# Writing out the first and last four turns of a software-pipelined kernel as one interleaved list per engine

## The chip, the cores and the metric

One core of one Trainium2 chip. The metric is device time in microseconds (us), from launch to the end of the program; the median over runs is what is compared.

## The reference

The input x is 32 sequences of 256 rows of 128 numbers, float32. Four layers follow each other, each as x = layer_norm(x + layer(x)):

```python
x = _layernorm(x + attn0(x))   # A: linear attention, 8 heads, RoPE, 5-tap conv of v, gate
x = _layernorm(x + ffn0(x))    # B: base matmul + the top-1 of four low-rank adapters
x = _layernorm(x + attn1(x))   # C: causal softmax attention, one head
x = _layernorm(x + ffn1(x))    # R, D: top-4 of 16 experts (grouped) + a shared expert, SwiGLU
```

## The kernel before, in words

The rows are cut into 16 blocks of 512 (two sequences, four tiles of 128 rows). Each block passes through the stages A, B, C and D; `r_` pieces (the router) belong to stage D's expert choice, and `e_norm` is the last layer norm with the store behind it. Each stage is split into small pieces, one function for each piece and engine: `a_xT_` to `a_out` are PE's pieces of stage A, `a_rope`, `conv_tap`, `a_mix`, `a_res` DVE's, and so on. A piece waits on semaphores for its inputs and for the buffers that it overwrites, then issues one to twelve instructions. The same name on two engines is one step seen from both.

The loop is software-pipelined over 20 turns. Turn i holds stage A of block i, B of i - 1 (with the projections of C), C and the router of i - 2, D of i - 3 and the last norm's input of i - 4. `turn(i)` exists once for each engine and lists the pieces in a fixed, hand-written order; `live(n)` leaves out pieces of blocks that don't exist. So turn 0 has A(0) alone, turn 1 A(1) and B(0), turn 2 A(2), B(1), C(0), turn 3 A(3), B(2), C(1), D(0); turns 4 to 15 are complete; turns 16 to 19 run empty again, down to the last norm of block 15. Everything is unrolled: there is no loop on the chip, and each engine works its list strictly in order.

Most buffers exist once. Stage A uses the PSUM banks A0 and A1, stages B, C and the router B0 and B1, stage D the banks GB (gate), UB (up), CB (routing weights) and YB (sum). So the next block's `a_xT_` waits for this block's `a_mix` (A0), its `a_vT_` for this block's `a_res` (A1). D's inner chain is, for chunk c of nine: `d_hidden` (six matmuls into GB and UB), `d_silu` on ACT, `d_gu` and `d_hid` on DVE, `d_down` on PE; a `d_hidden` waits for the `d_silu` and the `d_gu` of the chunk before.

POOL has the `ln_of(k, n)` pieces: eleven tiny instructions that make mean and rstd of layer norm k from DVE's statistics. `split_late` (ACT, then DVE) splits the expert weights into a high and a low part; it runs once, and D(0) needs it.

In the order before, POOL's `turn` puts `x0_lo(i)`, on which `a_vT_(i)` waits, ahead of `a_rope(i)`, but behind `ln_of(0, i - 1)` of the turn before; PE's puts `a_out(i)` behind `c_xT(i - 1)`, and `a_num_`, `a_aT`, `a_out` between the chunks of D:

```python
                if d: d_hidden(i - 3, 1 - odd, 8)
                if b: c_xT(i - 1)
                if a: a_out(i)
                if d: d_down(i - 3, 7)
                if b: c_project(i - 1)
```

Of the kernel before, what the change touches and what calls it, by code (L numbers as in the profile page):

```python
# [111 lines left out]
def build(nc, x_dram, weight_dram, whole_dram, out_dram):  # L112
    blocks = x_dram.shape[0] // BLOCK
    turns = blocks + 4
    assert blocks % 2 == 0
# [1162 lines left out]
```

## Time and profile before

| | us |
|---|---|
| median of 3 runs (lowest, highest) | 721.76 (721.19, 721.92) |
| profiled execution, its own time | 720.15 |
| span of the profile | 718.4 |
| busy: PE, DVE, ACT, POOL | 657.7, 586.9, 485.1, 308.9 |

The profiled execution lies 1.61 below the median, and 1.75 of its time lie outside the span (launch and end). The page cuts the span into 40 slices of 18 us; PE's row shows 3, 4, 6, 6, 6 and 7 tenths in the first six slices, 9 (90% or more) from there on, and 4 in the last. Turn boundaries can be read off PE's timeline: `c_value` is PE's last piece of a turn. Turn 3 ends at 142.1 and turn 15 at 619.6. The span therefore splits into a first part of 142.1 (turns 0 to 3), twelve steady turns of 477.5 together (39.79 each), and a last part of 98.8 (turns 16 to 19).

### The profile page before, as it was taken

The page shows a single profiled execution, that of the slowest core. Times are in us where ns is not written, and L with a number is a line of the kernel's source. Part 1 is how long each engine was busy: PE and PEld are TensorE (multiplying, and loading weights), DVE is VectorE, ACT ScalarE, POOL GpSimd, SP SyncE. Part 2 cuts the span into 40 slices and gives each one's busy share as a digit, 9 for nine tenths or more (in the row PEclk, how much of TensorE's full clock was granted, in tenths as well). Part 3 has the DMA queues.
Part 4 walks back from the last instruction along what each step waited for, and adds up shares of the span by engine and source line. Part 5 has one row for each costly group of instructions (what it writes and reads, how often), then busy time and mean ns, then how long its engine had stood idle before and what let it go on. Part 6 is the DMA issues. An engine that isn't in the chain of part 4 may idle for free.

```text
span 718.4 us, 11716 instructions
## 1 busy us (share of the span) xinstructions
PE 657.7 (92%) x3654; PEld 508.2 (71%) x3654; DVE 586.9 (82%) x1873; ACT 485.1 (68%) x978; POOL 308.9 (43%) x793
## 2 busy tenths in 40 slices
PE   3466679999999999999999999999999999999994
PEld 2354558787878777787878787787868787766652
DVE  1566778989898888989899888989898998877672
ACT  2233558587787878687787877786877868676623
POOL 1234443445453544536454535446454535250311
PEclk9787989999999999999999999999999999999997
DMA  6000000000000010101000000101000000000000
GB/s 227 15 1 16 1 16 0 16 1 16 16 16 16 1 31 1 31 1 30 1 17 16 10 21 2 30 1 31 2 28 3 16 1 1 15 1 16 16 1 29
DMA packets 18686, 12.69 MB, mean 18 GB/s; under 512 B 704, under 2 KB 18240, under 8 KB 18368
## 3 DMA queue, kind: packets, MB, share of 16 engines
q1 hardware_dynamic: 18624, 11.95, 5.4%
q8 instruction: 29, 0.48, 0.3%
q14 instruction: 33, 0.27, 0.1%
HBM read 7.75 MB, written 4.19 MB: 17 GB/s over the span
## 4 chain that ended last, share of the span: by engine, by line
PE 87%; DVE 5%; POOL 3%; ACT 3%; issue 1%; DMA 1%; SPq 0%; ACTq 0%; DVEq 0%; POOLq 0%
PE bank L551 17%; PE bank L346 11%; PE bank L348 10%; PE bank L347 10%; PE bank L355 10%; PE bank L461 2%; PE bank L434 2%; PE bank L472 2%; PE bank L478 2%; PE bank L473 2%; PE bank L406 2%; PE bank L518 2%; PE bank L449 2%; PE bank L424 2%; PE bank L505 1%; PE bank L499 1%
## 5 line engine op out<-in xcount | busy, mean ns | idle before, releaser
L551 PE MATMUL bank<-hid,whole 128*128 128x512 f32 x288 | 147.2, 593 | 0.8 <-DVE hid L1055 0.8
L346 PE MATMUL bank<-x3T_hi,w_hi 128*128 128x512 f32 x288 | 138.0, 479 | 1.8 <-DVE gu L1052 1.4
L728 ACT ACTIVATE silu<-bank 128x512 f32<-128x512 f32 x144 | 86.3, 600 | 66.1 <-PE bank L348 62.9
L1052 DVE TENSOR_TENSOR gu<-silu,bank 128x512 f32<-128x512 f32 x128 | 86.7, 677 | 35.3 <-ACT silu L728 18.8
L348 PE MATMUL bank<-x3T_hi,w_lo 128*128 128x512 f32 x288 | 113.5, 394 | 0.0
L347 PE MATMUL bank<-x3T_lo,w_hi 128*128 128x512 f32 x288 | 112.7, 391 | 0.0
L1151 POOL TENSOR_TENSOR moment<-stats 128x4 f32<-128x4 f32 x192 | 44.7, 265 | 149.3 <-DVE stats L866 133.8
L1062 DVE TENSOR_TENSOR hid<-gu,bank 128x512 f32<-128x512 f32 x128 | 87.2, 681 | 1.8 <-PE bank L551 0.8
L346 PEld LDWEIGHTS bank<-x3T_hi,w_hi 128*128 128x128 f32 x288 | 54.2, 188 | 30.8 <-ACT silu L728 9.8
L1137 POOL TENSOR_TENSOR qk<-rope_c,rope_s 128x512 f32<-128x512 f32 x32 | 40.6, 1279 | 80.8 <-DVE rope_s L828 80.8
L1151 POOL TENSOR_TENSOR rstd<-moment,whole 128x4 f32<-128x4 f32 x64 | 64.6, 1009 | 5.0
L347 PEld LDWEIGHTS bank<-x3T_lo,w_hi 128*128 128x128 f32 x288 | 54.5, 189 | 16.3 <-issue 10.0
L348 PEld LDWEIGHTS bank<-x3T_hi,w_lo 128*128 128x128 f32 x288 | 54.0, 188 | 12.2
L551 PEld LDWEIGHTS bank<-hid,whole 128*128 128x128 f32 x288 | 49.7, 189 | 15.3 <-issue 7.2
L1181 POOL TENSOR_TENSOR x3T_lo<-x3T,x3T_hi 128x512 fp32r<-128x512 f32 x16 | 22.0, 1372 | 87.9 <-ACT x3T_hi L718 87.9
L728 ACT ACT_TABLE_LOAD x45 | 57.7, 1283 | 0.8
L939 DVE SCALAR_TENSOR_TENSOR conv<-vT,whole,conv 128x512 f32<-128x512 f32 x64 | 54.3, 849 | 0.8
L866 DVE BATCH_NORM_STATS2 stats<-res 128x6 f32<-128x128 f32 x192 | 41.9, 281 | 1.7
L1151 POOL TENSOR_TENSOR moment<-moment,whole 128x4 f32<-128x4 f32 x192 | 35.2, 199 | 5.0
L355 PE MATMUL bank<-whole,x 128*128 128x128 f32 x192 | 30.0, 280 | 7.6 <-ACT x L634 7.2
L355 PEld LDWEIGHTS bank<-whole,x 128*128 128x128 f32 x192 | 23.7, 144 | 18.6 <-ACT x L634 8.1
L634 ACT ACTIVATE x<-bank,shift,rstd 128x128 f32<-128x128 f32 x64 | 24.1, 456 | 18.7 <-POOL shift L1151 18.7
(196 smaller groups left out, 1634.4 us busy)
## 6 DMA issues: line engine op xcount, KB each, us to landing
x_in<-x SPq DMA_DIRECT2D x16, 256.0 KB, 2.7
out<-x SPq DMA_DIRECT2D x16, 256.0 KB, 2.3
whole<-w_whole SPq DMA_DIRECT2D x1, 1198.5 KB, 5.4
w_raw<-w SPq DMA_DIRECT2D x1, 1152.0 KB
w_raw<-w SPq DMA_DIRECT2D x1, 546.0 KB, 6.7
whole<-w_whole SPq DMA_DIRECT2D x16, 32.0 KB
whole<-w_whole SPq DMA_DIRECT2D x1, 64.0 KB
```

The lines of the kernel that those rows point to most:

```text
L346: mm(out, wh, mh, start=True, stop=False)
L347: mm(out, wh, ml, start=False, stop=False)
L348: return mm(out, wl, mh, start=False, stop=True)
L355: last = nc.tensor.transpose(out[0:parts, t * P:(t + 1) * P], src(t), eye)
L551: mm(YB[:], whole[:, a:a + P], hid[:, c % 2], start=c == 0, stop=c == CHUNKS).then_inc(p_w2.sem, 1)
L728: fn(silu[:, c % 2], GB[:], ACT.Silu).then_inc(a_silu.sem, 1)
L866: nc.vector.bn_stats(stats[k][:, t, :], res[k][:, t, :]).then_inc(v_st[k].sem, 1)
L939: stt(conv[:], vT[:, :, j:j + SEQ], taps[:, j:j + 1], conv[:], ALU.mult, ALU.add).then_inc(v_conv.sem, 1)
L1052: tt(gu[:, c % 2], silu[:, c % 2], UB[:], ALU.mult).then_inc(v_gu.sem, 1)
L1062: tt(hid[:, c % 2], gu[:, c % 2], CB[:], ALU.mult).then_inc(v_hid.sem, 1)
L1137: tt(qk[:, 2 * h:2 * h + 2, :].rearrange("p t d -> p (t d)"), rope_c[:, h], rope_s[:, h], ALU.add).then_inc(g_qk.sem, 1)
L1151: tt(out, in0, in1, op).then_inc(g_ln[k].sem, 1)
```

## The change

The function `turn` stays as it is, but is called for turns 4 to 15 alone. Turns 0 to 3 are replaced on each engine by `first_turns()`, turns 16 to 19 by `last_turns()`: straight lists of the same pieces, each exactly once, in an order in which pieces of several blocks are mixed. No piece crosses from one of the three parts into another. PE's `a_qT_`, which reads what POOL's `a_rope` writes, gets a wait of its own, because in the new first list `a_qT_(2)` and `a_qT_(3)` stand ahead of `a_kv`, which had the wait before.

```diff
             def a_qT_(n):
                 pe.wait_ge(a_g.sem, a_g.at(n))
+                pe.wait_ge(g_qk.sem, g_qk.at(n))
                 transpose_tiles(A0, lambda t: qk[:, t, 0:P], ident).then_inc(p_qT.sem, 1)
...
-            for i in range(turns):
+            def first_turns():
+                a_xT_(0, 0, 0)
+                a_vT_(0)
+                a_qk(0)
...
+            def last_turns():
+                d_hidden(13, 1, 0)
+                c_scores(14)
...
+            first_turns()
+            for i in range(4, 16):
                 turn(i, i % 2, i // 2)
+            last_turns()
```

The lists themselves, in order, written without brackets: `d_hidden 0,2` is chunk 2 of block 0, `ln_of 2,0` the layer norm 2 of block 0; a name with several arguments is that piece called several times; the arguments that choose one of two buffers are left out.

```
PE first_turns (90 calls)
a_xT 0; a_vT 0; a_qk 0; a_g 0; a_v 0; a_kv 0; a_qT 0; a_num 0; a_aT 0; a_xT 1; a_out 0; a_vT 1; a_qk 1; b_xT 0;
b_small 0; a_v 1; a_g 1; a_kv 1; a_qT 1; a_num 1; b_dnT 0; b_up 0; a_aT 1; a_xT 2; a_out 1; c_xT 0; a_vT 2; c_project
0; c_value 0; c_scores 0; a_qk 2; c_pT 0; b_xT 1; c_av 0; a_g 2; a_qT 2; a_v 2; b_small 1; r_xT 0; a_kv 2; r_gate 0;
b_dnT 1; b_up 1; a_num 2; d_hidden 0,0; a_aT 2; d_hidden 0,1; a_xT 3; a_out 2; c_xT 1; c_project 1; c_value 1; a_vT 3;
a_qk 3; c_scores 1; d_cT 0; a_g 3; a_v 3; c_pT 1; d_down 0,0; c_av 1; a_qT 3; d_hidden 0,2; d_down 0,1; b_xT 2;
d_hidden 0,3; b_small 2; a_kv 3; d_down 0,2; r_xT 1; d_hidden 0,4; r_gate 1; d_down 0,3; d_hidden 0,5; a_num 3; b_dnT
2; d_hidden 0,6; b_up 2; d_down 0,4; d_hidden 0,7; a_aT 3; d_hidden 0,8; d_down 0,5 0,6; a_out 3; c_xT 2; d_down 0,7;
c_project 2; d_down 0,8; c_value 2
PE last_turns (78 calls)
d_hidden 13,0; c_scores 14; d_yT 12; d_cT 13; c_pT 14; d_hidden 13,1; c_av 14; b_xT 15; d_down 13,0; b_small 15;
d_hidden 13,2 13,3; d_down 13,1; d_hidden 13,4; r_xT 14; d_down 13,2; r_gate 14; d_down 13,3; d_hidden 13,5; b_dnT 15;
d_down 13,4; b_up 15; d_hidden 13,6; d_down 13,5; d_hidden 13,7; d_down 13,6; d_hidden 13,8; c_xT 15; d_down 13,7
13,8; d_hidden 14,0; c_project 15; c_value 15; d_hidden 14,1; c_scores 15; d_cT 14; d_yT 13; c_pT 15; d_down 14,0;
c_av 15; d_hidden 14,2; d_down 14,1; d_hidden 14,3; d_down 14,2; d_hidden 14,4; d_down 14,3; d_hidden 14,5; r_xT 15;
d_hidden 14,6; r_gate 15; d_down 14,4; d_hidden 14,7; d_down 14,5; d_hidden 14,8; d_down 14,6 14,7 14,8; d_hidden
15,0; d_yT 14; d_cT 15; d_hidden 15,1 15,2 15,3; d_down 15,0 15,1; d_hidden 15,4; d_down 15,2 15,3; d_hidden 15,5;
d_down 15,4; d_hidden 15,6; d_down 15,5; d_hidden 15,7; d_down 15,6; d_hidden 15,8; d_down 15,7 15,8; d_yT 15
ACT first_turns (66 calls)
x0_hi 0; a_vT 0; a_g 0; a_v 0; a_tap0 0; a_qT 0; x0_hi 1; a_vT 1; split_late; a_tap0 1; copy_xT 0,1; b_small 0; a_v 1;
a_g 1; b_exp 0; a_qT 1; b_dnT 0; b_layer_norm 0; x0_hi 2; copy_xT 0,2; c_qkv 0; a_vT 2; c_exp 0; c_pT 0; a_g 2; a_tap0
2; copy_xT 1,1; b_small 1; a_qT 2; a_v 2; c_norm 0; b_exp 1; r_hi 0; r_exp 0; b_dnT 1; d_silu 0,0; b_layer_norm 1;
x0_hi 3; copy_xT 1,2; d_silu 0,1; c_qkv 1; a_vT 3; a_tap0 3; c_exp 1; c_pT 1; a_g 3; d_silu 0,2; copy_xT 2,1; a_v 3;
d_silu 0,3; b_small 2; c_norm 1; a_qT 3; r_hi 1; d_silu 0,4; b_exp 2; r_exp 1; d_silu 0,5; b_dnT 2; d_silu 0,6 0,7;
b_layer_norm 2; copy_xT 2,2; d_silu 0,8; c_qkv 2; d_y 0
ACT last_turns (51 calls)
d_silu 13,0; c_exp 14; c_pT 14; d_silu 13,1; copy_xT 15,1; d_silu 13,2; b_small 15; e_norm 12; d_silu 13,3; c_norm 14;
d_silu 13,4; r_hi 14; r_exp 14; b_exp 15; d_silu 13,5; b_dnT 15; d_silu 13,6 13,7; b_layer_norm 15; d_silu 13,8;
copy_xT 15,2; d_silu 14,0; c_qkv 15; d_y 13; d_silu 14,1; c_exp 15; c_pT 15; d_silu 14,2 14,3 14,4; c_norm 15; d_silu
14,5; r_hi 15; d_silu 14,6; r_exp 15; d_silu 14,7 14,8 15,0; d_y 14; e_norm 13; d_silu 15,1 15,2 15,3 15,4 15,5;
e_norm 14; d_silu 15,6 15,7 15,8; d_y 15; e_norm 15
DVE first_turns (98 calls)
a_rope 0; conv_tap 0,1; a_kv 0; conv_tap 0,2 0,3; a_den 0; a_att 0; conv_tap 0,4; a_mix 0; a_res 0; a_layer_norm 0;
a_rope 1; b_norm 0,0 0,1; b_logits 0; b_first 0; a_kv 1; b_weigh 0; conv_tap 1,1 1,2 1,3 1,4; b_res 0; a_den 1; a_att
1; a_mix 1; a_res 1; split_late; c_value 0; c_max 0; a_layer_norm 1; a_rope 2; c_res 0; b_norm 1,0 1,1; b_logits 1;
conv_tap 2,1; b_first 1; b_weigh 1; conv_tap 2,2; r_groups 0,0; a_kv 2; r_groups 0,1; conv_tap 2,3; r_groups 0,2;
conv_tap 2,4; r_groups 0,3; b_res 1; a_den 2; a_att 2; d_gu 0,0; a_mix 2; r_groups 0,4; a_res 2; r_combine 0; c_value
1; a_rope 3; c_max 1; d_hid 0,0; d_gu 0,1; conv_tap 3,1 3,2; d_hid 0,1; a_layer_norm 2; c_res 1; d_gu 0,2; d_hid 0,2;
d_gu 0,3; d_hid 0,3; b_norm 2,0 2,1; conv_tap 3,3 3,4; a_kv 3; d_gu 0,4; b_logits 2; b_first 2; b_weigh 2; d_hid 0,4;
r_groups 1,0; d_gu 0,5; a_den 3; r_groups 1,1 1,2; d_hid 0,5; d_gu 0,6; b_res 2; a_att 3; d_hid 0,6; d_gu 0,7;
r_groups 1,3; a_mix 3; d_hid 0,7; r_groups 1,4; a_res 3; d_gu 0,8; r_combine 1; c_value 2
DVE last_turns (79 calls)
c_max 14; d_gu 13,0; d_res 12; d_hid 13,0; a_layer_norm 15; c_res 14; d_gu 13,1; d_hid 13,1; d_gu 13,2; d_hid 13,2;
b_norm 15,0; d_gu 13,3; b_norm 15,1; d_hid 13,3; b_logits 15; d_gu 13,4; d_hid 13,4; b_first 15; b_weigh 15; r_groups
14,0 14,1; d_gu 13,5; d_hid 13,5; b_res 15; d_gu 13,6; d_hid 13,6; d_gu 13,7; d_hid 13,7; r_groups 14,2 14,3; d_gu
13,8; r_groups 14,4; r_combine 14; d_gu 14,0; c_value 15; c_max 15; d_hid 14,0; d_res 13; d_gu 14,1; d_hid 14,1; c_res
15; d_gu 14,2; d_hid 14,2; d_gu 14,3; d_hid 14,3; d_gu 14,4; d_hid 14,4; d_gu 14,5; d_hid 14,5; d_gu 14,6; r_groups
15,0; d_hid 14,6; r_groups 15,1 15,2 15,3; d_gu 14,7; r_groups 15,4; d_hid 14,7; d_gu 14,8; r_combine 15; d_gu 15,0;
d_hid 15,0; d_gu 15,1; d_hid 15,1; d_gu 15,2; d_res 14; d_hid 15,2; d_gu 15,3; d_hid 15,3; d_gu 15,4; d_hid 15,4; d_gu
15,5; d_hid 15,5; d_gu 15,6; d_hid 15,6; d_gu 15,7; d_hid 15,7; d_gu 15,8; d_res 15
POOL first_turns (26 calls)
x0_lo 0; a_rope 0; a_gate 0; x0_lo 1; ln_of 0,0; a_rope 1; b_norm 0; ln_of 1,0; a_gate 1; x0_lo 2; ln_of 0,1; a_rope
2; ln_of 2,0; b_norm 1; x3_lo 0; ln_of 1,1; a_gate 2; x0_lo 3; ln_of 0,2; a_rope 3; ln_of 2,1; b_norm 2; x3_lo 1;
ln_of 1,2; a_gate 3; ln_of 0,3
POOL last_turns (10 calls)
ln_of 3,12 2,14; b_norm 15; ln_of 1,15; x3_lo 14; ln_of 2,15 3,13; x3_lo 15; ln_of 3,14 3,15
```

## Rows read from the trace of the kernel before

**Rows 1.** Busy time of each engine by stretch; x counts instructions, PEclk is the granted clock

```profile
0.00:32.70 32.70, 13.31 (x65) 10.94 (x66) 10.84 (x31) 7.93 (x18) 6.93 (x13) 0.93 0.37 125
32.70:67.30 34.60, 20.35 (x105) 15.99 (x104) 21.07 (x59) 12.70 (x28) 13.97 (x36) 0.72 0.06 16
67.30:102.10 34.80, 22.80 (x149) 18.59 (x147) 24.34 (x88) 16.06 (x42) 14.99 (x37) 0.90 0.03 8
102.10:142.10 40.00, 39.96 (x228) 31.00 (x228) 35.09 (x115) 30.03 (x58) 16.50 (x41) 1.00 0.03 8
...
142.10:619.60 477.50, 477.50 (x2737) 374.83 (x2736) 430.96 (x1393) 365.37 (x732) 233.09 (x589) 1.00 0.05 13
619.60:718.40 98.80, 83.77 (x380) 56.87 (x379) 64.55 (x189) 53.06 (x101) 23.40 (x81) 0.96 0.04 11
...
706.00:718.40 12.40, 2.36 (x8) 0.71 (x6) 2.08 (x6) 2.24 (x5) 2.76 (x11) 0.70 0.07 21
```

**Rows 2.** Who waited for whom, 0 to 142 us: total, times, longest

```profile
ACT x L634 <- POOL shift L1151: 13.2, 3, 6.9
```

**Rows 3.** POOL's timeline in turn 1

```profile
36.45 1.03 POOL L1151 TENSOR_TENSOR rstd<-moment,whole 128x4 f32<-128x4 f32 x1
37.45 1.26 POOL L1176 TENSOR_TENSOR x0T_lo<-x0T,x0T_hi 128x512 fp32r<-128x512 f32 x1
```

**Rows 4.** DVE's timeline in the first part: start, length, what

```profile
37.51 2.05 DVE L871 TENSOR_SCALAR x<-res,mean,rstd 128x128 f32<-128x128 f32 x4 [3.02 <-POOL rstd L1151]
41.73 0.69 DVE L826 TENSOR_TENSOR rope_c<-bank,whole 128x512 f32<-128x512 f32 x1 [2.16 <-PE bank L394]
...
56.93 0.88 DVE L859 SCALAR_TENSOR_TENSOR mixT<-bank,neg_mean,conv 128x256 f32<-128x256 f32 x2 [1.21 <-PE bank L355]
...
63.44 0.69 DVE L876 TENSOR_TENSOR res<-x_in,bank 128x512 f32<-128x512 f32 x1 [1.90 <-PE bank L434]
...
72.72 0.69 DVE L826 TENSOR_TENSOR rope_c<-bank,whole 128x512 f32<-128x512 f32 x1 [1.51 <-PE bank L394]
...
92.56 0.88 DVE L859 SCALAR_TENSOR_TENSOR mixT<-bank,neg_mean,conv 128x256 f32<-128x256 f32 x2
...
98.90 0.69 DVE L876 TENSOR_TENSOR res<-x_in,bank 128x512 f32<-128x512 f32 x1 [2.90 <-PE bank L434]
...
110.26 0.69 DVE L826 TENSOR_TENSOR rope_c<-bank,whole 128x512 f32<-128x512 f32 x1 [1.50 <-PE bank L394]
...
143.06 0.68 DVE L999 TENSOR_TENSOR cv<-bank,whole 128x512 f32<-128x512 f32 x1
```

**Rows 5.** PE's timeline in turns 1 and 3

```profile
38.76 0.79 PE L346 MATMUL bank<-x0T_hi,w_hi 128*128 128x512 f32 x1 [5.05 <-POOL x0T_lo L1176]
...
60.58 1.11 PE L355 MATMUL bank<-whole,x 128*128 128x128 f32 x4 [3.69 <-ACT x L634]
...
109.27 0.36 PE L392 MATMUL bank<-w_hi,x0T_hi 128*128 128x256 f32 x1
```

**Rows 6.** DVE's timeline, two operations that appear short and long

```profile
57.72 1.22 DVE L806 TENSOR_TENSOR w_lo<-w_raw,w_hi 128x1024 fp32r<-128x1024 f32 x1
...
59.05 2.29 DVE L806 TENSOR_TENSOR w_lo<-w_raw,w_hi 128x1024 fp32r<-128x1024 f32 x1
...
107.65 1.11 DVE L871 TENSOR_SCALAR x<-res,mean,rstd 128x128 f32<-128x128 f32 x4
```

**Rows 7.** PE's timeline in the last part

```profile
665.85 0.50 PE L346 MATMUL bank<-x3T_hi,w_hi 128*128 128x512 f32 x1 [1.23 <-DVE gu L1052]
...
687.15 0.66 PE L355 MATMUL bank<-whole,comb 128*128 128x128 f32 x4 [0.96 <-DVE comb L1045]
```

**Rows 8.** Groups of instructions: busy, mean ns, idle before and its releaser

```profile
L728 ACT ACT_TABLE_LOAD x45 | 57.7, 1283 | 0.8
...
L355 PE MATMUL bank<-whole,v_cent 128*128 128x128 f32 x64 | 9.9, 277 | 0.4 <-DVE rope_s L828 0.4
...
L355 PE MATMUL bank<-whole,qk 128*128 128x128 f32 x64 | 9.6, 273 | 0.0
```

More of the change, by code:

```diff
@@ L765, in turn, with first_turns @@
                 if d: d_y(i - 3)
-            for i in range(turns):
+            def first_turns():
+                x0_hi(0)
+                a_vT_(0)
+                a_g_(0)
+                a_v_(0)
+                a_tap0(0)
+                a_qT_(0)
+                x0_hi(1)
+                a_vT_(1)
+                split_late()
+                a_tap0(1)
+                copy_xT(0, 1, B0)
+                b_small(0)
+                a_v_(1)
+                a_g_(1)
+                b_exp(0)
+                a_qT_(1)
+                b_dnT(0)
+                b_layer_norm(0)
+                x0_hi(2)
+                copy_xT(0, 2, B0)
+                c_qkv(0)
+                a_vT_(2)
+                c_exp(0)
+                c_pT(0)
+                a_g_(2)
+                a_tap0(2)
+                copy_xT(1, 1, B0)
+                b_small(1)
+                a_qT_(2)
+                a_v_(2)
+                c_norm(0, 0)
+                b_exp(1)
+                r_hi(0, 0)
+                r_exp(0)
+                b_dnT(1)
+                d_silu(0, 0)
+                b_layer_norm(1)
+                x0_hi(3)
+                copy_xT(1, 2, B0)
+                d_silu(0, 1)
+                c_qkv(1)
+                a_vT_(3)
+                a_tap0(3)
+                c_exp(1)
+                c_pT(1)
+                a_g_(3)
+                d_silu(0, 2)
+                copy_xT(2, 1, B0)
+                a_v_(3)
+                d_silu(0, 3)
+                b_small(2)
+                c_norm(1, 1)
+                a_qT_(3)
+                r_hi(1, 1)
+                d_silu(0, 4)
+                b_exp(2)
+                r_exp(1)
+                d_silu(0, 5)
+                b_dnT(2)
+                d_silu(0, 6)
+                d_silu(0, 7)
+                b_layer_norm(2)
+                copy_xT(2, 2, B0)
+                d_silu(0, 8)
+                c_qkv(2)
+                d_y(0)
@@ L768, in _ @@
+            first_turns()
+            for i in range(4, 16):
                 turn(i, i % 2)
+            last_turns()
         @block.vector
@@ L1120, in _ @@
+            first_turns()
+            for i in range(4, 16):
                 turn(i, i % 2)
+            last_turns()
         @block.gpsimd
@@ L1193, in turn, with first_turns, last_turns @@
                 if a: ln_of(0, i)
-            for i in range(turns):
+            def first_turns():
+                x0_lo(0)
+                a_rope(0)
+                a_gate(0)
+                x0_lo(1)
+                ln_of(0, 0)
+                a_rope(1)
+                b_norm(0)
+                ln_of(1, 0)
+                a_gate(1)
+                x0_lo(2)
+                ln_of(0, 1)
+                a_rope(2)
+                ln_of(2, 0)
+                b_norm(1)
+                x3_lo(0, 0)
+                ln_of(1, 1)
+                a_gate(2)
+                x0_lo(3)
+                ln_of(0, 2)
+                a_rope(3)
+                ln_of(2, 1)
+                b_norm(2)
+                x3_lo(1, 1)
+                ln_of(1, 2)
+                a_gate(3)
+                ln_of(0, 3)
+            def last_turns():
+                ln_of(3, 12)
+                ln_of(2, 14)
+                b_norm(15)
+                ln_of(1, 15)
+                x3_lo(14, 0)
+                ln_of(2, 15)
+                ln_of(3, 13)
+                x3_lo(15, 1)
+                ln_of(3, 14)
+                ln_of(3, 15)
+            first_turns()
+            for i in range(4, 16):
                 turn(i, i % 2)
+            last_turns()
 def _constants():
```

395 lines of the change are left out of this document (394 added, 1 removed).

## The prediction

> **What bounds the kernel now.** Read the table by stretches first [rows 1]. In the twelve steady turns PE is busy for all of 477.5 us, at full clock. They keep their order, so nothing can be won there; the change must be judged in the two stretches around them. In the last 98.8 us PE is busy for 83.77, so it idles for 15.0. Of these 10.0 (12.40 less 2.36) lie in the very end, where block 15's sum goes through the last transposition, the layer norm and the store; no order shortens that. So the last part has little to give. The first 142.1 us are different: turns 0, 1 and 2 are 32.7, 34.6 and 34.8 us long, with PE busy for 13.31, 20.35 and 22.80, and DVE for 10.84, 21.07 and 24.34. No engine is the bound there. They are long because each engine walks its list in order and waits. Turn 3 (40.0 us) is full already: PE 39.96, DVE 35.09.
>
> The waits say for what [rows 2, 5]: in the first part ACT waits 13.2 us in three `b_layer_norm` for POOL's shift, and PE's matmuls of `a_vT_(1)` wait 5.05 for POOL's x0T_lo. Both are chains through POOL's small layer-norm instructions. What counts is whether such a chain holds up work that doesn't need it, by standing ahead of it in a list. I therefore walked through the new lists by hand, piece by piece on the four engines, with the durations of the trace, and compare six marks on DVE with before; DVE sees every step of stage A.
>
> **Turn 1.** Before, POOL does x0T_lo of block 1 right behind rstd of block 0, at 37.45 [rows 3], so `a_vT_(1)` starts at 38.76 [rows 5] and `a_rope(1)` at 41.73 [rows 4]. The new list of POOL has `x0_lo(1)` ahead of `ln_of(0, 0)`, and PE has `a_xT_(1)` ahead of `a_out(0)`; `a_vT_(1)` can go once block 0's `a_res` has freed A1, at about 32.8. But DVE keeps `a_layer_norm(0)` ahead of `a_rope(1)`, and that needs rstd. So the rope comes from this chain: rstd ends at 36.45 + 1.03 = 37.5, about 0.9 earlier since one conv tap has moved behind `a_att(0)`; then the norm, 1.11 where POOL is idle [rows 6]: 37.7, which is 4.0 earlier. From there to `a_mix(1)` took 15.2 (41.73 to 56.93) [rows 4]; I take 16.2, because ACT's `split_late` now stands ahead of `a_tap0(1)` and x1T's copy. Mix at 53.9, 3.0 earlier. Then the clear gain: PE had `a_out(1)` behind `c_xT(0)`, which waited 3.69 for the norm on ACT [rows 5], and `a_res(1)` came 6.5 after the mix [rows 4]. Now `a_out(1)` stands ahead and only POOL's norm and gate lie between: 4.0. `a_res(1)` at 57.9, 5.5 earlier.
>
> **Turn 2.** From `a_res(1)` to `a_rope(2)` took 9.3 (63.44 to 72.72) [rows 4]; now 10.3, because DVE's `split_late` and C(0)'s `c_value` and `c_max` stand between. Rope at 68.2, 4.5 earlier. From there to `a_mix(2)` took 19.8 and does again: B(1), the first router pieces and the conv taps are reordered, and `d_gu(0, 0)` is fitted in. Mix at 88.0, 4.6 earlier. `a_out(2)` is pulled ahead of `c_xT(1)` as in turn 1: `a_res` follows the mix after 3.85 instead of 6.34, at 91.85, 7.0 earlier.
>
> **Turn 3.** `a_rope(3)` came 11.36 after `a_res(2)` (98.90 to 110.26) [rows 4]; between stood the router's `r_combine(0)`, `c_value`, `d_gu`, `c_max`, `d_hid` and a layer norm. Now only the statistics (0.8), `r_combine(0)` (3.6) and `c_value(1)` (0.6) do: 5.8 with the start-ups. `a_vT_(3)` and `a_qk(3)` are done on PE by 98.2, so the rope goes at 97.65 on its first half, 12.6 earlier. From here both engines are nearly full. DVE: before, 33.5 from this rope to the end of `c_value(2)` (110.26 to 143.74) [rows 4]; to this come `c_max(1)`, `d_hid(0, 0)` and the norm of block 2, which were done before and now follow, 2.9 together; and I find 2.1 of waits more than before, at `d_gu(0, 3)`, `d_gu(0, 4)` (ACT's Silu behind `c_norm(1)`) and `d_hid(0, 7)`. 97.65 + 33.5 + 2.9 + 2.1 = 136.2 against 143.74: **7.5 earlier**. PE: 40.0 of turn 3, less what it has done by the end of `a_qk(3)`. Before, `a_qk(3)` starts 7.2 into the turn [rows 1, 5]; of that, 3.0 (`c_scores`, `d_cT`, `c_pT`) still lie ahead, and `a_qk` itself takes 1.5: 40.0 - 4.2 - 1.5 = 34.3, so PE can't end before 98.2 + 34.3 = 132.5, 9.6 earlier than 142.1. My walk puts its end at 134.0, 8.1 earlier. I take the later engine, 7.5. The steady turns then start 7.5 earlier and are what they were.
>
> **The last part.** Here PE has two waits of size, 1.23 for `d_gu` and 0.96 for `comb` of block 15 [rows 7]; by the walk the first goes, as `d_hidden(14, 0)` and `(14, 1)` now stand around C(15), and the second stays at about 0.5. Against it, `b_exp(15)` now stands behind `r_exp(14)`, which costs 0.4, and the router of block 15 comes one chunk later. Net 1.1 earlier; bounds 0 and 5.0 (15.0 less 10.0 that PE idles at the end).
>
> **Edits at nothing.** The added wait: in the steady turns `a_kv` stands ahead of `a_qT_` with the same count, so it is met when PE arrives; behind it stand the four transpositions and `d_hidden` 2 or 3. For its own price, the four transpositions of v_cent behind two waits take 277 ns each, those of qk behind one 273 [rows 8]: 12 turns x 4 x 0.004 = 0.2 us at most, and 0 is nearer, since a piece with a met wait shows no gap. If the cover were gone, the wait would be for POOL's two additions; in `first_turns` it is really waited for, and the walk has it. Exp and Silu now change places less often: I count 7 table loads in turn 3 and 10 in the last part before, 5 and 8 after. Four loads of 1283 ns [rows 8] are 5.1 us of ACT, hidden as ACT is busy 30.03 of 40.0 in turn 3 [rows 1]; at most the 1.0 of the wait at `d_gu(0, 4)` would come back without them.
>
> **The sum.** 7.5 + 1.1 = 8.6. Against the profiled execution: 720.15 - 8.6 = 711.6. That execution lay 1.61 below the median, so the median comes to 721.76 - 8.6 = **713.2**.
>
> **Rivals.**
> - *DVE gets slower where it is packed* (0.20). Some DVE operations appear short and long: the layer norm's four 1.11 and, beside x0T_lo on POOL, 2.05; the split 1.22 and, beside POOL's product oT, 2.29 [rows 3, 4, 6]. I took the short ones. If the two norms that were short and the first half of the split meet POOL's large additions, that is 2 x 0.94 + 1.07 = 3.0 on DVE's path: gain 5.6, time 716.2. For it: POOL has more to do in the same time. Against: behind `ln_of` in POOL's list mostly a wait follows. The Trainium skill (GPSIMD Engine Reference, section Specifications) says that GpSimd shares SBUF interfaces with VectorE, with contention for VectorE instructions with two SBUF inputs or in a 2-port mode. The trace agrees for these two operations, with 2.05 against 1.11 and 2.29 against 1.22.
> - *The last part fills up too* (0.08): 7.5 + 5.0 = 12.5, time 709.3. Against it: D's chunks hang on each other there and nothing else is left to put between.
> - *Given back in turn 3* (0.06). The lead of 12.6 at `a_rope(3)` is worth only what PE and DVE can take up; if DVE waits for 9 us there instead of 2.1, say because each Silu of D(0) sits on ACT behind a norm or an Exp that is late, the first part wins 0.6: about 720.5 to 722, no change.
> - *Slower: the clock* (0.04). Turns 1 and 2 ran at a granted clock of 0.72 and 0.90, with PE busy for 59 and 66% [rows 1]. If D(0), taken apart among waits, ran at 0.72, PE's 34.3 would take 47.6 and end at 145.8: 3.7 later, less 1.1, time 724.4. It decides from a clock below 0.76 in this stretch. Against: turn 3 ran at 1.00, and by the walk PE is busy for 34.3 of 35.8 us.
>
> **How the numbers follow.** The forecast, a gain of 6.5 to 11, has 0.62, and its own range is 710.8 to 715.3. A measurement of this kernel can tell 0.2%, 1.4 us. Faster by more: 0.62 + 0.20 + 0.08 = 0.90; within: 0.06; slower: 0.04. For 8 in 10 the range goes up past the first rival, to 718.5, and down nearly to the second, to 709.0; the rest lies outside.
>
> **What will show it.** On DVE `a_res(1)` near 58, `a_res(2)` near 92, `a_rope(3)` near 98, `c_value(2)` ending near 136; PE's `c_value(2)` ending near 134, the twelve steady turns at 477.5, and 97.7 behind them. 86 table loads in place of 90. The prediction is wrong if `a_rope(2)` isn't earlier than 71 (the pieces put ahead of it cost more than the waits that they fill), if DVE waits more than 5 us between `a_rope(3)` and `c_value(2)`, or if the steady turns lengthen.

## The result, and the profile after

The changed kernel takes 709.65 us (median of 4 runs, 707.79 to 711.87) beside 721.48 for the kernel before (720.89 to 721.92): a ratio of 0.9838, 95% interval 0.9805 to 0.9871. The profiled execution took 708.59 us, with a span of 706.8.

Marked by the end of PE's `c_value`, which closes a turn, the two spans compare like this:

| stretch | before | after | gain | predicted |
|---|---|---|---|---|
| start to the end of `c_value(2)` | 142.09 | 133.09 | 9.00 | 7.5 |
| to the end of `c_value(14)` (twelve steady turns) | 477.50 | 477.63 | -0.13 | 0 |
| to the end of the last `d_down` | 88.11 | 85.43 | 2.68 | 1.1 |
| the very end | 10.66 | 10.65 | 0.01 | 0 |
| span | 718.4 | 706.8 | 11.6 | 8.6 |

The first row rests on PE's `c_value(2)`, before and after; a matmul group's start plus its length is its end:

```profile
141.04 1.05 PE L478 MATMUL bank<-w_raw,x2T 128*128 128x128 f32 x8
```

```profile
132.04 1.05 PE L479 MATMUL bank<-w_raw,x2T 128*128 128x128 f32 x8
```

The windows of the changed kernel answer to [rows 1]; columns as there.

```profile
28.00:55.20 27.20, 18.90 (x86) 16.03 (x86) 15.02 (x51) 9.45 (x21) 10.80 (x25) 0.69 0.04 11
55.20:91.40 36.20, 29.04 (x174) 24.19 (x175) 26.87 (x84) 20.16 (x49) 19.37 (x41) 0.83 0.03 8
91.40:132.93 41.53, 40.25 (x225) 29.76 (x223) 37.03 (x128) 26.79 (x56) 18.04 (x48) 1.00 0.05 14
132.93:610.49 477.56, 477.56 (x2739) 374.76 (x2737) 431.35 (x1394) 365.32 (x732) 232.81 (x589) 1.00 0.05 13
```

From 91 us on PE is nearly full, earlier than before. Ahead of it, in 63.4 us, it is busy for 47.94 and at a granted clock of 0.69 and 0.83, lower than turns 1 and 2 had before (0.72 and 0.90). The busy time there is partly slow time. Over the whole first part the two profiles are alike in this: the mean granted clock is 0.89 in 142.09 us before and 0.88 in 133.09 us after, so about 31 us at half clock (0.50, the lower of the two levels in the records; the other is 1.00) in either. Less time at half clock is not where the gain comes from; where that time falls is taken up below.

DVE's timeline of the changed kernel, the marks of [rows 4]:

```profile
37.04 1.12 DVE L1169 TENSOR_SCALAR x<-res,mean,rstd 128x128 f32<-128x128 f32 x4 [3.02 <-POOL rstd L1632]
38.07 0.68 DVE L1124 TENSOR_TENSOR rope_c<-bank,whole 128x512 f32<-128x512 f32 x1
...
55.16 0.88 DVE L1157 SCALAR_TENSOR_TENSOR mixT<-bank,neg_mean,conv 128x256 f32<-128x256 f32 x2 [1.15 <-PE bank L355]
59.56 0.69 DVE L1174 TENSOR_TENSOR res<-x_in,bank 128x512 f32<-128x512 f32 x1 [3.52 <-PE bank L435]
...
67.85 0.68 DVE L1124 TENSOR_TENSOR rope_c<-bank,whole 128x512 f32<-128x512 f32 x1
...
87.84 0.88 DVE L1157 SCALAR_TENSOR_TENSOR mixT<-bank,neg_mean,conv 128x256 f32<-128x256 f32 x2
...
91.43 0.69 DVE L1174 TENSOR_TENSOR res<-x_in,bank 128x512 f32<-128x512 f32 x1 [0.18 <-PE bank L435]
...
97.05 0.68 DVE L1124 TENSOR_TENSOR rope_c<-bank,whole 128x512 f32<-128x512 f32 x1
...
134.41 0.68 DVE L1297 TENSOR_TENSOR cv<-bank,whole 128x512 f32<-128x512 f32 x1
```

| mark | before | predicted | after |
|---|---|---|---|
| `a_rope(1)` | 41.73 | 37.7 | 38.07 |
| `a_mix(1)` | 56.93 | 53.9 | 55.16 |
| `a_res(1)` | 63.44 | 57.9 | 59.56 |
| `a_rope(2)` | 72.72 | 68.2 | 67.85 |
| `a_mix(2)` | 92.56 | 88.0 | 87.84 |
| `a_res(2)` | 98.90 | 91.85 | 91.43 |
| `a_rope(3)` | 110.26 | 97.65 | 97.05 |
| `c_value(2)` on DVE ends | 143.74 | 136.2 | 135.09 |
| `c_value(2)` on PE ends | 142.09 | 134.0 | 133.09 |

In the last part the 1.23 at `d_gu` and the 0.96 at `comb` of [rows 7] are gone. Five waits of PE are left ahead of the very end, the largest 0.48, the others 0.31 to 0.34; two of them:

```profile
671.08 1.98 PE L552 MATMUL bank<-hid,whole 128*128 128x512 f32 x4 [0.34 <-DVE hid L1360]
...
674.92 0.66 PE L355 MATMUL bank<-whole,yT 128*128 128x128 f32 x4 [0.48 <-ACT yT L907]
```

The runs of the changed kernel lie 4 us apart, those of the kernel before that were timed with it 1 us; over all sets below the latter go from 720.9 to 723.4. The runs go with their mean granted clock, which the experiments take up.

### The profile page after: what moved, and what is told of

It is laid out like the page before. It is cut to its first block, busy times and chain, and to the rows that moved or that the text cites. A ratio compares the mean times of both kernels' runs of the same rounds, so it can differ in the third digit from the quotient of the medians.

```text
span 706.8 us, 11728 instructions
## 1 busy us (share of the span) xinstructions
PE 662.7 (94%) x3654; PEld 510.9 (72%) x3654; DVE 585.6 (83%) x1873; ACT 479.4 (68%) x974; POOL 310.7 (44%) x793
## 4 chain that ended last, share of the span: by engine, by line
PE 88%; ACT 4%; DVE 3%; POOL 2%; issue 1%; DMA 1%; SPq 0%; ACTq 0%; DVEq 0%; POOLq 0%
PE bank L552 17%; PE bank L346 11%; PE bank L348 10%; PE bank L347 10%; PE bank L355 10%; PE bank L462 2%; PE bank L435 2%; PE bank L406 2%; PE bank L479 2%; PE bank L425 2%; PE bank L473 2%; PE bank L474 2%; PE bank L450 2%; PE bank L519 2%; PE bank L500 1%; PE bank L506 1%
## 5 line engine op out<-in xcount | busy, mean ns | idle before, releaser
L1632 POOL TENSOR_TENSOR moment<-stats 128x4 f32<-128x4 f32 x192 | 46.5, 274 | 151.9 <-DVE stats L1164 124.6
L552 PEld LDWEIGHTS bank<-hid,whole 128*128 128x128 f32 x288 | 49.5, 189 | 16.2 <-issue 7.4
L1657 POOL TENSOR_TENSOR x0T_lo<-x0T,x0T_hi 128x512 fp32r<-128x512 f32 x16 | 20.3, 1270 | 36.6 <-ACT x0T L815 36.6
```

Of the source, the lines that this page charges most:

```text
L552: mm(YB[:], whole[:, a:a + P], hid[:, c % 2], start=c == 0, stop=c == CHUNKS).then_inc(p_w2.sem, 1)
L1632: tt(out, in0, in1, op).then_inc(g_ln[k].sem, 1)
```

## The experiments

Each experiment was timed against the kernel before on the same chip, in five sets. The medians of the kernel before in these sets lie between 721.5 and 722.3, so a comparison with the 709.65 of the changed kernel, which belongs to another set, is uncertain by some 0.8 us beside the spread of the runs.

**The two halves by themselves.** `first_only`:

```diff
-            for i in range(4, 16):
+            for i in range(4, turns):
...
-            last_turns()
```

> The new lists for turns 0 to 3, the old order in the last four turns. By the two profiles PE's c_value(2) ends 9.1 us earlier in the first part, the steady turns are 0.3 longer, and the last part gives 2.7: this kernel then is 9.1 - 0.3 = 8.9 us faster than the kernel before (712.6 beside 721.5), with the last part at 99.1 us again. The rival is the prediction's own sum, 7.5 for the first part; what is above it in the profile would belong to a good moment of the granted clock, and this kernel would come out at 714.0.

Measured: 710.27 us (710.20 to 711.21) beside 721.62, ratio 0.9841 (0.9828 to 0.9855). Its profiled execution took 711.21 us, 8.9 less than that of the kernel before (720.15), as expected: `c_value(2)` ends at 133.01, the last part takes 88.14. But the kernel's other runs lie 0.9 us below its profiled one, and those of the kernel before 1.0 to 3.0 above its own, so the medians differ by 11.4. The median itself, 710.27, is 2.3 below the expected 712.6. The first part is worth 8.9 in one pair of profiles and 11.4 in the medians; the rival's 7.5 is below both.

`last_only`:

```diff
-            first_turns()
-            for i in range(4, 16):
+            for i in range(16):
```

> The old order in turns 0 to 15 (with the added wait in each a_qT_), the new list for the last four turns. By the two profiles the last part goes from 99.05 to 96.3 us, since PE's waits there for block 14's and 15's pieces go from 5.0 to 1.8: 2.7 us faster than before, 718.8. The rival is the prediction's 1.1, 720.4; then the rest of the 2.7 would come from how the lists of the first part meet those of the last, or from the clock.

Measured: 718.61 us (718.45 to 720.34) beside 721.62, ratio 0.9959 (0.9946 to 0.9973), 3.0 us faster; the last part takes 85.35 in its profile. The 2.7 belong to the new list of the last four turns, whatever stands ahead of it. In the eleven profiles with that list unchanged the part takes 85.32 to 85.43. This profile shows one thing more: its turns 0 to 3 are in the old order, as in the kernel before, and yet its `c_value(2)` ends at 143.11, 1.0 later. The mean clock of that stretch is 0.87, beside 0.89:

```profile
0.00:143.11 143.11, 98.37 (x540) 78.65 (x541) 91.45 (x293) 66.72 (x145) 51.88 (x125) 0.87 0.12 37
```

So the profile of the kernel before, with its 142.09, was one of its quicker executions.

**The added wait.** `wait_four`:

```diff
-                pe.wait_ge(g_qk.sem, g_qk.at(n))
+                if n < 4: pe.wait_ge(g_qk.sem, g_qk.at(n))
```

> The whole change, but with the added wait in a_qT_ for blocks 0 to 3 alone, so that the twelve steady turns are as they were. By the prediction the added wait costs nothing there: the time is that of the changed kernel, 709.7, within 0.2, apart from the spread of the runs. The rival takes the 0.26 us by which the steady turns of the changed kernel were longer as the price of twelve waits: 0.3 less. It is also a second sample of the changed kernel: if its runs spread over 4 us too and lie higher where the mean granted clock is lower, the spread belongs to the new lists and not to one bad run.

Measured: 708.44 us (706.09 to 711.59), ratio 0.9812 (0.9789 to 0.9836). From the end of `c_value(2)` to that of `c_value(14)` it takes 477.58, with the twelve waits 477.63. A price of 0.05 can't be told from none: the other profiles with the twelve waits take 477.50 to 477.70, the kernel before without them 477.50. Its five runs, with the four of the changed kernel, form one series of mean granted clock and time: 0.983: 706.09; 0.978: 707.36, 707.79; 0.975: 708.44; 0.973: 708.48, 708.59; 0.971: 710.71; 0.969: 711.59, 711.87. So the 4 us of the changed kernel were not one bad run, and they go with the clock. That is a correlation; what the clock costs is tried below, by holding it. Nor is all of the spread new: the kernel before has 2.1 us in this set (721.10 to 723.17).

**Is it the chain, or the pieces of turn 3 put into turn 2?** `turn3_old` takes out of the four lists what belongs to turn 3 and runs that turn by the old loop:

```diff
-                d_hidden(0, 0, 0)
                 a_aT(2)
-                d_hidden(0, 0, 1)
-                a_xT_(3, 1, 1)
                 a_out(2)
                 c_xT(1)
...
-            for i in range(4, 16):
+            for i in range(3, 16):
```

> The new lists for turns 0 to 2 without any piece of turn 3, then turn 3 in the old order, and the new last four turns. By the prediction's steps block 2's a_res is still about 7 us earlier than before (near 91.5), and PE then has the 40.0 us of turn 3 whole, from about 95.5: c_value(2) ends near 135.6 in place of 132.9, so 2.7 later than the changed kernel, near 712.3. The rival: the early gaps were worth little by themselves, and the gain of the first part is that D(0) and A(3) are mixed into turn 2; then half or more of it is lost, 4.5 us or more, 714 and up.

Measured: 713.65 us (712.56 to 713.85) beside 721.62. `a_res(2)` is at 91.85, where it should be, but PE's `c_value(2)` ends at 138.32, 5.2 later than in the changed kernel, where the prediction's steps give 2.7: by the profiles it is the rival's number. The medians lie 4.0 apart, between the two. PE's timeline of this kernel shows why:

```profile
86.65 0.65 PE L355 MATMUL bank<-whole,att 128*128 128x128 f32 x4 [1.44 <-DVE att L1080]
89.74 2.08 PE L435 MATMUL bank<-whole,oT 128*128 128x128 f32 x8 [2.43 <-POOL oT L1512]
...
93.35 2.07 PE L473 MATMUL bank<-x2T,w_raw 128*128 128x512 f32 x2 [0.69 <-ACT x2T L762]
95.22 1.91 PE L474 MATMUL bank<-x2T,w_raw 128*128 128x512 f32 x2
96.92 1.61 PE L479 MATMUL bank<-w_raw,x2T 128*128 128x128 f32 x8
```

Its window from 91.4 to 98.5 has a granted clock of 0.53:

```profile
91.40:98.50 7.10, 6.41 (x20) 3.90 (x20) 4.74 (x22) 2.60 (x4) 2.62 (x10) 0.53 0.14 38
```

Where D(0)'s matmuls stood, PE now waits for 1.44 and 2.43, and then `a_out(2)` to `c_value(1)` run at half clock, 89.74 to 98.53, 8.8 us; in the changed kernel 90.24 to 95.58, 5.3:

```profile
90.24 1.16 PE L435 MATMUL bank<-whole,oT 128*128 128x128 f32 x8 [0.62 <-POOL oT L1624]
...
94.42 1.16 PE L479 MATMUL bank<-w_raw,x2T 128*128 128x128 f32 x8
```

Whether the clock or the missing work costs the 5.2 was tried next: `turn3_warm` puts work into those waits that serves nothing, here against `turn3_old`.

```diff
+            def warm(k):
+                for _ in range(k):
+                    nc.tensor.transpose(GB[:, 0:P], ident, ident)
...
+                warm(5)
                 a_aT(2)
+                warm(9)
                 a_out(2)
                 c_xT(1)
+                warm(2)
                 c_project(1)
```

> The kernel with turn 3 in the old order (713.65 us), and 16 extra transpositions of the identity into an unused bank, put into PE's list ahead of block 2's a_aT (5), a_out (9) and C(1)'s c_project (2), where PE waited 1.44, 2.43 and 0.69 us. They do no work of the kernel. If the 3.4 us by which a_out(2) to c_value(1) took longer there (8.8 against 5.3 in the changed kernel) came from the granted clock (0.53 in that stretch), which fell because PE had nothing to do in those waits, then those pieces now run at full clock, c_value(1) ends near 95 in place of 98.5, and the time is about 710.2. The rival: what was lost was D(0)'s and A(3)'s work itself, filling the waits; then idle transpositions bring nothing and the time is 713.6 or more.

Measured: 711.05 us (710.67 to 713.43), 2.6 below `turn3_old` and nearer to the expected 710.2 than to the rival's 713.6. The same pieces on PE:

```profile
90.64 1.16 PE L439 MATMUL bank<-whole,oT 128*128 128x128 f32 x8 [1.32 <-POOL oT L1519]
...
92.92 1.12 PE L477 MATMUL bank<-x2T,w_raw 128*128 128x512 f32 x2 [0.47 <-ACT x2T L769]
93.89 1.02 PE L478 MATMUL bank<-x2T,w_raw 128*128 128x512 f32 x2
94.83 1.16 PE L483 MATMUL bank<-w_raw,x2T 128*128 128x128 f32 x8
```

They take 5.35 us, the expected 3.4 less; 1.0 is given back because `a_mix(2)` came 1.0 later in this run (88.37 against 87.34). `c_value(2)` ends at 135.80, 2.5 earlier than in `turn3_old`. So of the 5.2, 2.5 came back with the clock in these profiles, and 3.4 would have without that delay: half to two thirds is the clock that D(0)'s early matmuls held up. That the rest is the work itself is what remains by subtraction; no run shows it.

**Single moves undone.** `out_behind`:

```diff
-                a_out(1)
                 c_xT(0)
+                a_out(1)
...
-                a_out(2)
                 c_xT(1)
+                a_out(2)
```

> The whole change, but with a_out(1) back behind c_xT(0) and a_out(2) back behind c_xT(1) on PE. By the prediction each of these moves brought about 2.5 us at the next a_res, so both a_res are late, block 1's by 2.5 (62.1) and block 2's by 5 (96.4), and the time is some 4 us longer, 713.6. The rival, from the profile of the changed kernel: ACT's norm for c_xT(0) ends at 57.45 there and POOL's product for a_out(1) at 57.39, and likewise at 90.5 and 90.2 in turn 2, so that the swap costs only the four transpositions, about 1.0 and 0.7: a_res at 60.6 and 93.1, the time 1 to 1.7 longer.

Measured: 712.61 us (709.04 to 714.75); runs so far apart can't decide between 713.6 and the rival's 710.7 to 711.4, the marks can. From `a_mix` to `a_res` it takes 4.87 and 4.39, in the changed kernel 4.40 and 3.59: the moves are worth 0.5 and 0.8, not 2.5 each. The profile is nevertheless 4.5 later at `c_value(2)`, since `a_mix(2)`, ahead of the second swap, comes at 91.55 instead of 87.84. Both kernels wait 3.6 us at `r_xT(0)`, to 78.0 and 77.9, and in both the clock falls. The window of `out_behind` in which it is low:

```profile
76.50:90.10 13.60, 11.42 (x48) 10.68 (x49) 9.51 (x35) 4.79 (x11) 3.91 (x12) 0.50 0.00 0
```

and that of the changed kernel:

```profile
74.70:81.50 6.80, 3.56 (x17) 3.56 (x17) 5.05 (x21) 3.86 (x9) 3.52 (x4) 0.50 0.00 0
```

The clock is at half for 13.6 us in one execution and for 6.8 in the other, where half of it falls into the wait. The same pieces behind the same wait therefore run at half clock for 12.1 us in one and 3.6 in the other. The 3.7 by which `a_mix(2)` is later are about what the runs of the changed kernel lie apart (4.1).

`lo_behind`, on POOL:

```diff
-                x0_lo(1)
                 ln_of(0, 0)
+                x0_lo(1)
...
```

and likewise `x0_lo(2)`, `x0_lo(3)` behind `ln_of(0, 1)`, `ln_of(0, 2)`.

> The whole change, but on POOL x0T_lo of blocks 1, 2 and 3 back behind the layer norm of the block before. By the prediction's first step POOL's order sets a_rope(1): x0T_lo then runs at 37.0 instead of 31.4, a_vT(1) starts 5 us later, at 38.3, a_rope(1) 3 us later, near 41, and in turn 2 a_vT(2) goes from 60.4 to about 66 with the pieces of C(0) queued behind it, a_rope(2) near 76, and the time 7 to 8.5 us longer, about 717.5: most of the gain is gone. The rival: the rope waits for POOL's rstd in any case and the rest is taken up by slack, so that only the 3 us of turn 1 are lost, 712.7.

Measured: 726.85 us (724.26 to 728.76), ratio 1.0069 (1.0045 to 1.0094): slower than the kernel before, and 9 us beyond the expected 717.5: neither number was near. `a_rope(1)` comes at 42.59, 4.5 later than in the changed kernel, `a_rope(2)` at 82.23, 14.4 later. Its POOL, PE and DVE timelines, one fence each:

```profile
71.20 1.01 POOL L1632 TENSOR_TENSOR rstd<-moment,whole 128x4 f32<-128x4 f32 x1
72.18 1.26 POOL L1657 TENSOR_TENSOR x0T_lo<-x0T,x0T_hi 128x512 fp32r<-128x512 f32 x1
```

```profile
73.50 0.79 PE L346 MATMUL bank<-x0T_hi,w_hi 128*128 128x512 f32 x1 [6.96 <-POOL x0T_lo L1657]
```

```profile
78.82 0.69 DVE L1297 TENSOR_TENSOR cv<-bank,whole 128x512 f32<-128x512 f32 x1 [8.85 <-PE bank L479]
```

Read from the top: POOL finishes the norm of block 1 before it makes x0T_lo of block 2; PE has `a_vT(2)` ahead of C(0) and waits 6.96; DVE has C(0)'s `c_value` ahead of the norm that block 1 needs and waits 8.85. In this kernel the new orders of PE and DVE only pay with POOL's. The clock has a part in it (0.961 to 0.966 in these runs, 0.969 to 0.978 in those of the changed kernel); how large, no run shows.

**The last part.** `last_av`:

```diff
                 c_pT(14)
+                c_av(14)
                 d_hidden(13, 1, 1)
-                c_av(14)
...
                 c_pT(15)
+                c_av(15)
                 d_down(14, 0)
-                c_av(15)
```

> The whole change, but in the last four turns c_av(14) and c_av(15) back directly behind c_pT(14) and c_pT(15) on PE, without d_hidden(13, 1) and d_down(14, 0) between them. Before, PE waited 0.63 us at each of the two; the prediction had only counted the waits of 1.23 and 0.96. If the 2.7 us of the last part are the sum of such small waits that got filled, these two come back: the last part (end of c_value(14) to the end of the last d_down, 85.3 to 85.4 us in the four profiles of the new list, 88.1 in two of the old one) becomes about 86.6, 1.2 longer. The rival: a wait that is opened here is made up at the next piece that waits for another engine, and the part stays within 0.3 of 85.4; then the 2.7 come from C(15) standing earlier as a whole.

Measured: 709.17 us (708.79 to 713.17); the times can't tell 1 us here, the profile can. The last part takes 86.80, 1.4 longer, and two waits stand in PE's timeline that the changed kernel doesn't have:

```profile
616.11 0.49 PE L506 MATMUL bank<-cv,probT 128*128 128x128 f32 x2 [0.58 <-ACT probT L874]
...
652.87 0.49 PE L506 MATMUL bank<-cv,probT 128*128 128x128 f32 x2 [0.58 <-ACT probT L874]
```

What is opened there is not made up later, and the rival's 0.3 is out.

**Further by order.** `tight` puts the nineteen pieces around turn 2 into another order on PE, and their partners elsewhere. The core on PE, without the lines that go further down in exchange:

```diff
                 a_v_(2)
+                a_qT_(2)
+                a_kv(2)
+                a_num_(2)
                 r_xT(0, 0)
+                a_aT(2)
...
                 b_up(1)
+                a_out(2)
                 d_hidden(0, 0, 1)
+                a_vT_(3)
+                a_qk(3)
                 c_xT(1)
```

> The whole change, and in turn 2 the pieces are moved further: on PE a_kv(2) and a_num(2) ahead of r_xT(0), into the wait of 3.62 us there, a_out(2), a_vT(3) and a_qk(3) ahead of c_xT(1); on ACT x1T's copy ahead of a_g(2) and x0T_hi(3) ahead of the Silus; on DVE block 2's kv_m, den and att ahead of b_logits(1) with the conv taps in its waits, and a_rope(3) ahead of c_value(1); on POOL a_gate(2) and x0T_lo(3) ahead of the norm of x1(1). If the chain of stage A through turn 2 is what holds the first part, a_mix(2) goes from 87.8 to about 81 and a_rope(3) from 97 to about 91; from there PE is the bound, which idled some 7 us between 55 and 91 and ran at a clock of 0.83, so 3 to 4 us come out at the end: about 706. The rival: B(1), which is now behind, arrives 2 us later at c_xT(1), PE waits there instead, and the time is the changed kernel's, 709 to 710, or up to 2 worse.

Measured: 711.21 us (710.49 to 712.01). The rival holds. `a_mix(2)` is at 81.31 as meant, but `a_rope(3)` only at 95.86: DVE waits 3.69 for `b_up(1)`, which now stands behind the first `d_hidden`, and the window from 80 to 88 has a clock of 0.62. B(1) is late for `c_xT(1)`, and behind that wait the clock falls once more, to 0.57 from 96 to 100. Its PE:

```profile
94.40 0.66 PE L355 MATMUL bank<-whole,x 128*128 128x128 f32 x4 [1.60 <-ACT x L809]
```

`c_value(2)` ends at 135.16, 2.1 later than in the changed kernel.

**Further by the clock.** `warm` puts the idle transpositions of `turn3_warm` into the changed kernel: `warm(2)` to `warm(12)` ahead of fourteen pieces that wait in turns 0 to 2.

> The whole change, and 57 extra transpositions of the identity into an unused bank, 2 to 12 in each of fourteen waits of PE in turns 0 to 2. They do no work of the kernel. If the granted clock (0.69 from 28 to 55 us and 0.83 from there to 91) is a price that the first part still pays, the pieces on the chain (a_out, a_vT, a_qk, a_kv of blocks 1 and 2) take half the time there: block 2's a_res 4 to 5 us earlier, near 87, the time near 705.5, and the runs closer together than 4 us, since the spread (706.1 at a mean clock of 0.983, 711.9 at 0.969) is the clock's. The rival: the chain is set by POOL's and DVE's small steps, PE's excess is hidden behind them, and the transpositions stand ahead of pieces that could have gone; no change or up to 1 us slower, with the same spread.

Measured: 709.38 us (705.50 to 709.86), the rival's number. Block 2's `a_rope` is at 64.99, 2.9 earlier, but `a_mix(2)` at 87.90 and `a_res(2)` at 92.29: the lead is lost between 65 and 88 us, where the clock fell again; the rival's reason is not needed. The waits were filled by a third only, as one transposition takes 0.12 us. `warm_full` has 141 of them:

```diff
+                warm(28)
                 r_xT(0, 0)
...
```

> The whole change with 141 idle transpositions in place of the 57 of the kernel with extra transpositions in turns 0 to 2. There one took 0.12 us at full clock, not 0.22, so the waits were only partly filled; the clock stayed at 1.00 until 37 us, block 2's a_rope came 2.9 us earlier, and then it fell again, at 37 us behind a wait of 1.80 that was left and at 76 us behind one of 2.30, and between a_rope(2) and a_mix(2) the lead was lost. Now each wait is filled to about its length. If the idle waits are what lets the clock fall, it stays near 1.00 through both stretches, block 2's a_res comes near 87 in place of 91.4, the steady turns start 3 to 4 us earlier and the time is about 705.5, with runs within 2 us of each other. The rival: the clock falls all the same, or the transpositions overrun the waits and stand ahead of work that is ready; then the time is 709 or more and this way of holding the clock is worth nothing here.

Measured: 707.02 us (705.97 to 708.96), ratio 0.9793 (0.9773 to 0.9813), between the two numbers expected. `a_rope(2)` is at 64.20, `a_res(2)` again at 91.34. The windows show the one drop that was left, behind waits of 0.56, 0.25 and 0.68, though PE is then busy for 6.80 of 7.00:

```profile
76.00:79.00 3.00, 2.14 (x16) 1.81 (x16) 2.93 (x10) 0.75 (x3) 1.27 (x1) 1.00 0.00 0
79.00:86.00 7.00, 6.80 (x26) 6.33 (x27) 4.35 (x16) 2.03 (x3) 2.58 (x11) 0.51 0.00 0
```

`warm_more` has 177 and fills those as well.

> As the kernel with 141 idle transpositions, with 177: the waits that were left there are filled too (1.64 ahead of a_num(1), 0.70 ahead of b_xT(0), and 0.56, 0.25 and 0.68 ahead of r_xT(0), r_gate(0) and b_dnT(1), behind which the clock fell from 79 to 86 us). If the waits let the clock fall, this last drop goes too: b_up(1), a_num(2) and the first D(0) matmuls take half as long, block 2's a_res comes near 88 in place of 91.3, and the time is about 704.5. The rival: the clock falls at that point whatever PE does in the waits (every profile so far has such a drop between 72 and 90 us), and the time stays at 707.

Measured: 704.64 us (704.37 to 705.89), ratio 0.9763 (0.9744 to 0.9781), five runs within 1.5 us. `a_res(2)` is at 87.52, `c_value(2)` ends at 129.20. The windows of this kernel:

```profile
28.00:52.80 24.80, 22.72 (x175) 19.63 (x174) 15.91 (x52) 9.36 (x21) 11.32 (x26) 1.00 0.04 12
52.80:87.50 34.70, 33.27 (x242) 28.23 (x243) 25.97 (x82) 20.20 (x49) 18.92 (x40) 1.00 0.03 9
...
76.00:79.00 3.00, 2.88 (x23) 2.37 (x22) 2.93 (x9) 0.74 (x3) 1.27 (x1) 1.00 0.00 0
79.00:86.00 7.00, 6.79 (x46) 5.79 (x45) 6.77 (x22) 2.95 (x6) 3.73 (x12) 1.00 0.01 2
```

In the same 7.00 us DVE now does 6.77 of work instead of 4.35: it had been waiting for slow matmuls. This version is faster than both kernels, by 17.3 us against before and 5.0 against the median of the changed one (3.8 against that of `wait_four`), and it does more work than either. Not tried: the same transpositions in the kernel before. How much of the gain of the new lists would be left if the clock were held in both is therefore not known.

## Why the prediction was right, and where it was off

**The number**: 713.2 was forecast and 709.65 measured, a gain of 11.8 where the sum had 8.6. That lies within the range of 709.0 to 718.5, near its lower end, and outside the forecast's own 710.8 to 715.3. It lies 0.4 from the 709.3 of the rival that the last part fills up too, but not for its reason: that part gave 2.7, not 5.0, and the rest came from the first. That the range, drawn down to that rival, reached the measured time is luck.

**What bounds it**: right. The steady turns stayed at 477.6, the gain lies in the two stretches around them. None of the prediction's signs of being wrong showed: `a_rope(2)` came at 67.85 (limit 71), DVE waited 3.0 us behind `a_rope(3)` (limit 5), and the steady turns lengthened by no more than profiles differ.

**Turn 1**: right in its chain. `a_rope(1)` came 3.7 earlier (predicted 4.0), by POOL's order: with x0T_lo put back it is at 42.59. `a_mix(1)` and `a_res(1)` came 1.3 and 1.7 later than forecast; PE ran from 40 to 48 us at 0.57. From `a_rope(1)` to `a_mix(1)` took 17.1 (forecast 16.2), in `warm_full`, at full clock there, 15.1: the clock costs 2.0, and the prediction had no term for it.

**"Now `a_out(1)` stands ahead and only POOL's norm and gate lie between"**: the interval shrank as predicted, from 6.5 to 4.4 and from 6.34 to 3.59, but not by that move. `out_behind` gives 0.5 and 0.8 for it. The rest comes from the other lists: ACT's norm for `c_xT` ends when POOL's product does (57.45 and 57.39), so `c_xT` no longer makes `a_out` wait.

**Turns 2 and 3**: right in their marks, within 0.6 us, but partly by errors that cancel. `a_res(1)` was 1.7 late, and from it to `a_rope(2)` took 8.3 instead of 10.3, as DVE's waits for PE there fell from 4.7 to 1.2. `a_rope(3)` at 97.05 is 13.2 earlier. Behind it DVE waits 1.20 and 0.56 at `d_gu` and 1.05 at `d_hid`, where the prediction had them, and needs 38.0 us to the end of `c_value(2)`, forecast 38.5. The lead at a mark alone is not the gain, though: in `turn3_old` `a_res(2)` is 7.0 earlier than before, as predicted, and PE's `c_value(2)` only 3.8. The rest of the 9.0 needs the pieces of turn 3 among those of turn 2.

**"I take the later engine, 7.5"**: this is the mis-sized term of the first part. DVE itself ended 8.65 earlier, 1.1 more than forecast (0.6 of it at `a_rope(3)`, 0.5 behind it). And the steady turn begins on PE, which ended 9.00 earlier; that DVE trailed it by 2.0 (1.65 before) cost at most the 0.13 by which the steady turns are longer. PE came within 0.6 of the bound of the same paragraph, 132.5.

**The last part, 1.1**: mis-sized, 2.7. The prediction counted "two waits of size". PE's waits sum to 4.97 us ahead of the very end before, and to 1.82 after. Of the kernel before, these went too:

```profile
626.31 0.49 PE L505 MATMUL bank<-cv,probT 128*128 128x128 f32 x2 [0.63 <-ACT probT L699]
...
638.66 0.50 PE L346 MATMUL bank<-x3T_hi,w_hi 128*128 128x512 f32 x1 [0.39 <-ACT silu L728]
...
661.46 0.49 PE L505 MATMUL bank<-cv,probT 128*128 128x128 f32 x2 [0.63 <-ACT probT L699]
...
683.67 1.13 PE L551 MATMUL bank<-hid,whole 128*128 128x512 f32 x2 [0.79 <-DVE hid L1055]
```

Of the 3.15, 2.68 show in the time. `last_av` shows that such a wait is worth its whole length, where PE is otherwise full: two of 0.58 cost 1.4.

**Edits at nothing**: right. The wait costs no more than profiles of the same list differ by; table loads fell from 90 to 86.

**The rivals.** DVE did not get slower where it matters: both norms kept 1.11 to 1.12 and the split 1.21. It was POOL that gave way there (below). Two other DVE operations did get longer beside POOL, by 1.05 at 80.34 and 0.94 at 89.09; PE waited for neither. The clock was judged by the wrong sign: as a loss in D(0), with 0.04. D(0) ran at 1.00 from 91.4 us on, and its early matmuls hold the clock up. Ahead of it the first part ran at half clock in places, as before, and the changed kernel still pays for that: 3.9 us between its profile and that of `warm_more` at `c_value(2)`, 5.0 between the medians. The price of "given back in turn 3" is a slip of the sum: 0.6 and 1.1 give 720.1, not 720.5 to 722.

What stays open: part of the 2.4 us between the profiles and the medians of `first_only`. The old first part in `last_only`, 1.0 longer at a lower clock, shows that the profile of the kernel before was a quick execution. For the other 1.4 the clock is a likely cause, but no profile shows it.

## What to carry to other kernels

Where one engine is full, each of its waits is worth its length, however small: sum them all before judging a stretch. Where it is not full, look at the granted clock beside the busy share: here real work moved into a wait paid twice, for itself and for the clock of what follows, and idle matmuls paid too, once they filled the waits. A move on one engine's list may be worthless or ruinous without its partners on the others, so undo single moves before saying which one paid.

## What was not expected of the hardware

**The clock.** The same pieces behind the same wait of 3.6 us ran at half clock for 3.6 us in one execution and for 12.1 in another. In `warm_full` the clock fell though no wait of PE from 46 us on was longer than 0.68, and it was at 0.51 for 7 us while PE was busy for 97% of them. The Trainium skill (TensorE: Matmul & The Clock Gate, section What's actually happening) says that the gate follows how busy PE has recently been, and that a kernel's number of slow matmuls varies from run to run. The runs agree in both: with the waits filled (`warm_more`) the clock stayed at 1.00, and equal pieces ran slow for unequal times. Why it stayed low for 7 us with PE busy, no run shows.

**POOL against DVE.** The layer norm of block 1 on POOL, in the changed kernel, and DVE's split beside it:

```profile
61.23 2.45 POOL L1632 TENSOR_TENSOR moment<-stats 128x4 f32<-128x4 f32 x3 [1.40 <-DVE stats L1164]
```

```profile
61.07 1.21 DVE L1104 TENSOR_TENSOR w_lo<-w_raw,w_hi 128x1024 fp32r<-128x1024 f32 x1
...
62.41 1.21 DVE L1104 TENSOR_TENSOR w_lo<-w_raw,w_hi 128x1024 fp32r<-128x1024 f32 x1
...
80.34 1.79 DVE L1237 SCALAR_TENSOR_TENSOR conv<-vT,whole,conv 128x512 f32<-128x512 f32 x1
```

POOL's three tiny operations take 2.45 us beside the split that started first, and 0.51 to 0.57 elsewhere. At 80.34 it is the other way round: POOL's x3T_lo starts at 80.32 and takes its usual 1.26, and the conv tap beside it takes 1.79 instead of 0.74. The Trainium skill (SBUF — State Buffer, section SBUF: two separate sides) says that the port pair of the two is an exclusive lock, held by whichever starts first, among others for a DVE operation with two inputs in SBUF. Both DVE operations here have two, and both cases agree with it.
